# Moving the subtraction that makes the low part of x from VectorE's queue to GpSimd's, among the norm chains

## The reference

```
qkv  = normalize_weight(w_proj) applied to x          # 1x1 projection, 512 -> 1536
q, k = pixnorm(q) * scale, pixnorm(k) * scale          # norm over the 64 values of a head
v    = pixnorm(v)
attn = softmax(q . k) over the 1024 pixels             # 8 heads
res  = normalize_weight(w_out) applied to (attn . v)
out  = (0.7 * x + 0.3 * res) / sqrt(0.7^2 + 0.3^2)
```

## Time and profile before

| | before |
|---|---|
| median of 3 runs | 2981.16 us (2980.13 to 2982.64) |
| the profiled execution's own time | 2980.2 us |
| its span, first to last instruction | 2978.4 us |
| granted PE clock, mean | 0.998 |
| busy share PE / DVE / ACT / POOL | 98% / 91% / 80% / 16% |

### The profile page before, as it was taken

One profiled execution on the slowest core, in us unless ns is written; L12 is line 12 of the kernel. 1 busy time (PEld: TensorE's weight loads), 2 busy tenths in 40 slices (PEclk: granted clock), 3 DMA queues, 4 the chain that ended last, 5 costly groups with the idle time before them and its releaser, 6 DMA issues.

```text
span 2978.4 us, 73541 instructions
## 1 busy us (share of the span) xinstructions
PE 2922.6 (98%) x30784; PEld 1989.4 (67%) x30784; DVE 2704.3 (91%) x3581; ACT 2375.3 (80%) x2993; POOL 481.8 (16%) x678
## 2 busy tenths in 40 slices
PE   7999999999999999999999999999999999999987
PEld 6666666766666666666676766666676666666654
DVE  6998999989989899899998999999998998989887
ACT  6887887878778777887877878788787877878775
POOL 0211121112111121112111211112111211112110
PEclk9999999999999999999999999999999999999999
DMA  4222324323242331433324233232432323223233
GB/s 106 51 51 61 83 47 100 58 61 79 54 97 62 68 86 37 93 69 75 72 49 98 51 79 76 58 86 48 100 58 61 79 54 97 56 74 72 51 72 93
DMA packets 459484, 210.28 MB, mean 71 GB/s; under 512 B 407952, under 2 KB 407952, under 8 KB 459152
## 3 DMA queue, kind: packets, MB, share of 16 engines
q1 hardware_dynamic: 459152, 205.58, 31.4%
HBM read 71.30 MB, written 33.55 MB: 35 GB/s over the span
## 4 chain that ended last, share of the span: by engine, by line
PE 61%; DVE 26%; POOL 5%; issue 5%; DMA 1%; SPq 0%; ACT 0%; DVEq 0%; POOLq 0%; ACTq 0%
PE ps_pv L987 14%; PE ps_score L964 13%; DVE probs L784 12%; PE ps_dense L942 9%; PE ps_dense L946 8%; PE ps_dense L944 8%; DVE probs L775 4%; PE ps_dense L1003 3%; PE ps_dense L1005 3%; PE ps_dense L1004 3%; DVE arena L746 3%; DVE sumsq L722 2%; DVE res_split L812 1%; POOL rs L453 1%; POOL rs_t L449 1%
## 5 line engine op out<-in xcount | busy, mean ns | idle before, releaser
L600 ACT ACTIVATE e_tile<-ps_score,shift 128x1024 f32<-128x1024 f32 x1024 | 1113.9, 1116 | 177.9 <-PE ps_score L964 158.8
L784 DVE TENSOR_TENSOR probs<-e_tile,probs 128x1024 f16<-128x1024 f32 x1024 | 1240.6, 1234 | 6.2 <-ACT probs L607 2.9
L987 PEld LDWEIGHTS ps_pv<-v_pair,probs 128*128 128x128 f16 x18432 | 737.1, 97 | 201.5 <-issue 142.4
L987 PE MATMUL ps_pv<-v_pair,probs 128*128 128x65 f16 (+2 forms) x18432 | 806.4, 202 | 15.2 <-DVE probs L784 6.3
L964 PE MATMUL ps_score<-qkT 64*128 64x512 f16 x6144 | 753.4, 378 | 3.4 <-ACT e_tile L600 3.3
L942 PE MATMUL ps_dense<-wpT_hi,x_hi 128*128 128x512 f32 x1536 | 635.5, 414 | 5.0 <-DVE wpT_lo L863 1.5
L946 PE MATMUL ps_dense<-wpT_hi,x_lo 128*128 128x512 f32 x1536 | 601.4, 392 | 0.0
L944 PE MATMUL ps_dense<-wpT_lo,x_hi 128*128 128x512 f32 x1536 | 599.0, 390 | 0.0
L607 ACT ACTIVATE probs<-e_tile 128x1024 f16<-128x1024 f32 x512 | 539.8, 1058 | 25.9 <-PE ps_pv L987 13.7
L964 PEld LDWEIGHTS ps_score<-qkT 64*128 64x128 f16 x6144 | 257.2, 94 | 362.9 <-issue 93.9
L775 DVE CAST probs<-e_tile 128x1024 f16<-128x1024 f32 x512 | 361.2, 706 | 101.7 <-PE ps_pv L987 83.5
(11 more groups left out here) (53 smaller groups left out, 1916.6 us busy)
## 6 DMA issues: line engine op xcount, KB each, us to landing
x_raw<-in_x SPq DMA_DIRECT2D x128, 256.0 KB, 3.4
x_res<-in_x SPq DMA_DIRECT2D x128, 256.0 KB, 3.0
out<-x_res SPq DMA_DIRECT2D x128, 256.0 KB, 2.3
arena<-in_w_proj SPq DMA_DIRECT2D x24, 128.0 KB, 3.6
qkT<-arena SPq DMA_TRANSPOSE x128, 4.5
resT<-res_split SPq DMA_TRANSPOSE x128, 3.2
arena<-in_w_out SPq DMA_DIRECT2D x1, 1024.0 KB, 8.5
```

The lines of the kernel that those rows point to most:

```text
L600: act.activation(e_tile[:, t % E_BUFS, :, :], ps_score[:, t % 2, :, :], ACT.Exp, bias=shift[:, 0:1], scale=1.0 / (QK_UP * QK_UP)).then_inc ...
L784: dve.tensor_tensor(probs_of(b, t, 1), e_tile[:, t % E_BUFS, :, :], probs_of(b, t, 0), ALU.subtract).then_inc(probs_low, 1)
L987: mm = pe.matmul(ps_pv[:, h, at_col:at_col + n], probs_of(b, t, part)[:, h, queries], v[:, cols], start=(j == 0 and it == 0 and part == 0 ...
```

## The change

POOL gets the function `split_x` and the table `LOW_X_AT` with its ticks unchanged; DVE loses both. The norm chains' ticks on POOL are set to those of DVE's seeds, so that POOL's queue has a norm chain at the place, among the subtractions, at which DVE's queue has its seed. Where two tasks of POOL have the same tick, the subtraction comes first.

```diff
 # STEADY
     "SEED_AT": (-15456, 3584, 23312),
-    "NORM_AT": (-17392, 5408, 33248),
+    "NORM_AT": (-15456, 3584, 23312),
 # FIRST
     "SEED_AT": (15712, 16304, 23312),
-    "NORM_AT": (33216, 33232, 33248),
+    "NORM_AT": (15712, 16304, 23312),
 # LAST
     "SEED_AT": (-14048, 4648, 24311),
-    "NORM_AT": (-32272, -32256, -32240),
+    "NORM_AT": (-14048, 4648, 24311),
...
 # in POOL's block
+            def split_x(b, piece):
+
+                n = 8 * b + piece
+                ct, half = X_PIECES[piece]
+                cols = slice(half * NH, (half + 1) * NH)
+                pool.wait_ge(x_high, n + 1)
+                pool.tensor_tensor(x_lo[:, ct, cols], x_raw[:, piece % 2, :],
+                                  x_hi[:, ct, cols].bitcast(F32), ALU.subtract).then_inc(x_split, 1)
+
             pool.wait_ge(consts_set, CONSTS)
-            names = dict(norm="NORM_AT")
+            names = dict(norm="NORM_AT",
+                         low_x="LOW_X_AT")
 
             def task(b, s, when):
+                for piece in when["low_x"].get(s, ()):
+                    split_x(b, piece)
                 for g in when["norm"].get(s, ()):
                     norms(b, g)
...
 # in DVE's block: split_x, its table and its loop are gone
-            def split_x(b, piece):
...
-                dve.wait_ge(x_high, n + 1)
-                dve.tensor_tensor(x_lo[:, ct, cols], x_raw[:, piece % 2, :],
-                                  x_hi[:, ct, cols].bitcast(F32), ALU.subtract).then_inc(x_split, 1)
...
-                         low_x="LOW_X_AT",
...
-                for piece in when["low_x"].get(s, ()):
-                    split_x(b, piece)
```

More of the change, by code:

```diff
@@ L705, in _ @@
             RSQRT_STEPS = 10
-            def split_x(b, piece):
-                n = 8 * b + piece
-                ct, half = X_PIECES[piece]
-                cols = slice(half * NH, (half + 1) * NH)
-                dve.wait_ge(x_high, n + 1)
-                dve.tensor_tensor(x_lo[:, ct, cols], x_raw[:, piece % 2, :],
-                                  x_hi[:, ct, cols].bitcast(F32), ALU.subtract).then_inc(x_split, 1)
             def reduce(b, n):
```

## The result

The changed kernel takes 3055.70 us (median of 4 runs, 3041.70 to 3060.83) against 2980.64 us: ratio 1.0243, 95% interval 1.0208 to 1.0278. It is 75 us slower, where 44 were forecast.

The account below looks back on a forecast made before the run. PE was taken to bound the kernel, busy 181.59 of 182.00 us an image. 2980.2 us plus 44.9 of waits at 15 passages, less 1 at the start, gave 3024.1; forecast 3025 us (+1.5%), range 2999 to 3054.

Parts of the forecast that it names:

- What bounds the kernel: PE, busy 181.59 of 182.00 us in a steady image, pays a new wait in its queue nearly in full.
- The order: On POOL, piece 3 stands behind group 2's norm chain, which ends 3.07 us after PE reaches the next image's tile 0.
- The earlier chain: Without piece 2's subtraction on DVE, the seed before POOL's norm chain comes 0.6 us earlier at each passage between images.
- The subtraction: Piece 3's 128x512 subtraction on POOL takes 1.1 us, bounds 0.65 and 2.3, plus 0.2 around it.
- The rule of GpSimd at twice VectorE's time: Rule against the change: piece 3 on POOL would take an estimated 1.4 us, making the sum 4.5 us higher.
- DVE's load: DVE loses 77 us of issue time; blocking by POOL's subtractions, at most 2.7 us more an image, fits its room: 0.
- The port rival: POOL's subtractions stop DVE instructions that PE needs: 56 us on top, 3081 us (3091 by the lock rule); chance 0.08.
- Sum: Whole execution: 2980.2 + 44.9 - 1 = 3024.1 us, with 2.9 us of wait a passage; forecast 3025 us.
- The start of image 0: Eight subtractions leave DVE's ramp, where PE does not bind: -1 us, 4.8 at most.
- Faster: No stall at tile 0, as the chain takes 7.7 us or less: 2974 us; chance 0.04.
- half the stall: The chain shortens by 2 to 3 us instead of 0.9, stall at tile 0 1.4 us x 15: 3001 us; chance 0.14.
- no effect: No stall appears, since PE's tile 0 is later held by something else anyway: 2981 us; chance 0.02.

Follow-up runs that it names:

- the 90 added subtractions: Changed kernel with pieces 0, 1, 2, 5, 6 and 7 subtracted twice on POOL in images 1 to 15: 3063.61 us, ratio 1.0275.
- the improved order: Changed kernel with the norm chain of group 2 one place later on POOL, behind piece 3 of the next image: 2992.83 us, ratio 1.0041.
- The chain of 10 instructions: Changed kernel with two Newton steps instead of three in POOL's norm chains, 10 instructions instead of 14: 2991.00 us, ratio 1.0035.

## Why the prediction was right in its mechanism and short in its size

*What bounds the kernel.* Right. PE took nearly all of the new wait: tile 0 came 3.4 us late at a passage, and a steady image without the low clock grew from 182.0 to 185.0 us, with PE busy for 181.7 of them, as I had said.

*The order.* Right. The waits name POOL's `x_lo` 15 times, as said, and putting piece 3 in front of the chain takes 63 of the 75 us away.

*The earlier chain.* I put the seed 0.6 us earlier. Measured against PE's arrival it was 865.88 - 857.18 = 8.70 us ahead before, and from the trace after 884.12 - 875.18 = 8.94 us ahead (884.12 is 0.03 us behind the start of the last output matmul, as before), so 0.24 us earlier. The chain went from 11.49 to 10.82 us: 0.67 instead of 0.9. Together the chain ended 2.16 us behind PE's arrival where I had 1.57. This is why the wait was longer than forecast: 3.4 us at a passage instead of 2.9.

*The subtraction.* I took 1.1 us plus 0.2 around it, out of bounds of 0.65 and 2.3. From the chain's end to tile 0 passed 887.55 - 886.28 = 1.27 us. That term holds. As an instruction it lasts 1.3 us when DVE leaves it alone and 1.55 on average. The rule of GpSimd at twice VectorE's time (Trainium skill, GPSIMD Engine Reference, section 4.1) fits that: 1.55 against 0.705 us, 2.2 times. It did not decide.

*DVE's load.* I expected that a subtraction on POOL may hold DVE for 0.94 us, and that it costs nothing. I put DVE's busy share at about 87%, and it was 89%: its busy time rose by 25.3 us though the subtractions' 77 us of issue time left, (25.3 + 77) / 128 = 0.80 us each. Two scalings beside two subtractions took 4.41 us instead of 2.36, 1.03 us each, of the subtraction's 1.3. The timelines of DVE and POOL in the changed kernel, one instruction a row:

```profile
886.24 1.26 POOL L464 TENSOR_TENSOR x_lo<-x_raw,x_hi 128x512 fp32r<-128x512 f32 x1
886.38 2.20 DVE L749 TENSOR_TENSOR arena<-arena,rs 128x1024 f32<-128x1024 f32 x1 [1.05 <-POOL rs L455]
...
887.46 2.26 POOL L464 TENSOR_TENSOR x_lo<-x_raw,x_hi 128x512 fp32r<-128x512 f32 x1
888.50 2.29 DVE L749 TENSOR_TENSOR arena<-arena,rs 128x1024 f32<-128x1024 f32 x1
```

They take turns. The first scaling starts 0.14 us behind the first subtraction and ends 1.08 us behind its end; the second subtraction ends 1.14 us behind that scaling, and the second scaling 1.07 us behind that subtraction. Each does nearly its whole work after the other has ended. This fits the lock for the whole instruction (Trainium skill, SBUF — State Buffer, section SBUF: two separate sides): a scaling is held for what is left of the subtraction when it starts, so for 1.0 to 1.1 us of the 1.3. The 0.12 us of the earlier trace rows, which I set against that rule, came from DVE instructions of another kind, with one input, which met POOL instructions that were over 0.25 us later, so it could not speak against it. The port rival's mechanism is there, then, but not its price: in the changed kernel it is hidden, as the 90 added subtractions show. Its one real cost was about 10 of the 12 us in the improved order, where it hit a residual addition that PE waits for.

*Sum.* The forecast had 44.9 us of waits; 50.1 were measured. The term that is missing, and the larger part of the error, is the clock. I looked at the granted clock before, saw 1.00 in the image, and did not ask what an idle PE would do to it. The runs price it at 24 us (3055.7 - 3031.8; by the two ratios, whose runs before were others, 21 us). 50 + 21 to 24 is 71 to 74 of the 75 us. My range ended at 3054, 2 us under the measured median; by the ratio, 1.0243 x 2981.16 = 3053.6, the time lies just inside it. That it comes so near is luck: the top of the range was room for a slow subtraction and a wait for DVE, neither of which came, and not for the clock.

*The start of image 0.* I gave it -1. The first tile 0 after it came at 147.28 instead of 140.17, 7.1 us later with a wait of 6.8: nothing was gained.

*The rivals.* Faster, half the stall and no effect are out. The faster one asked for a chain of 7.7 us or less. The chain of 10 instructions took 7.56, and the time was still 10 us above the kernel before, since the subtraction behind it took 2.24 us and not the 1.1 that the rival counted on.

## What to carry to other kernels

When work moves to an idle engine, don't sum its free time: write out its new queue and ask, for each item, which long chain now stands in front of it and who waits for it. An engine that is 98% busy pays nearly all of a new wait, and TensorE may pay for it again, since its clock can be lower behind the wait (24 us here, on top of 50). The repair can be as small as one place in a queue: here 63 of 75 us.

## What the runs showed of the hardware that I had not expected

A wait of about 3 us in PE's queue, once in 185 us, lowers the granted clock behind it in most cases and not in all: in the profiled execution of the changed kernel it fell at 11 of the 15 passages. Those at 516.5, 701.6 and 1260.7 us kept the full clock, behind the same wait of 3.08 us as the one at 887.6. What tells them apart I have not found out. In the run with the chain of 10 instructions the 14 waits of 0.5 to 1.0 us left the clock up, and the one of 5.4 us was followed by the low clock. The changed kernel's time varies with its clock: its four runs were 3041.7, 3053.4, 3058.0 and 3060.8 us with mean clocks of 0.992, 0.987, 0.986 and 0.984, while the kernel before stays within 3 us. Twelve matmuls on data of no use in the wait bring back about 24 us and, with 3 us, the narrow spread.

POOL's 128x512 subtraction holds a DVE instruction with two SBUF inputs that starts 0.14 us behind it for about 1.0 us of its 1.3, and a subtraction that meets such an instruction is lengthened in its turn, from 1.3 to 2.26 us.
